# Moving 50 bfloat16 transposes of a gated attention and FFN block from TensorE to the DMA queue

## The chip, the cores and the metric

The kernel runs on one core of a Trainium2 chip. The metric is the device time of one execution in microseconds (us); before the change it is 677.74 us, the median of 3 runs that lie between 677.37 and 677.95. Engines are called as the profile calls them: PE is the matrix engine (PEld its weight loads), DVE the vector engine, ACT the scalar engine, POOL the general engine GpSimd. SP only issues DMAs here; ACT issues some too.

## The reference

The block takes x, 2 x 2048 tokens of 512 floats, and adds two gated branches. Cut to what matters:

```
x = x + tanh(g_xattn) * xattn(layernorm(x), ctx, mask, Wq, Wk, Wv, Wo)     # 16 heads, 77 keys
x = x + tanh(g_ffn)   * ffn(layernorm(x), clip_x, clip_down, w_gate, w_up, w_down)

def weight_fake_quant(w):           # one scale per row
    scale = max(abs(w), axis=1) / 127
    return clip(round(w / scale), -128, 127) * scale
def act_fake_quant(x, clip):        # one scale for the whole tensor
    scale = sigmoid(clip) * max(abs(x)) / 127
    return clip(round(x / scale), -128, 127) * scale
def ffn(x):
    xq   = act_fake_quant(x, clip_x)
    gate = xq @ weight_fake_quant(w_gate).T       # w_gate, w_up: 1408 x 512
    up   = xq @ weight_fake_quant(w_up).T
    h    = act_fake_quant(silu(gate) * up, clip_down)
    return h @ weight_fake_quant(w_down).T
```

The quantised integers are exact in bfloat16, so the matrix products of the FFN run on bfloat16 copies of them and the scales are put in afterwards.

## The kernel before

The tokens are 32 tiles of 128 rows, and x stays in SBUF (`x1`). The program is three blocks one after the other, each with its engines' instruction streams written out by hand, ordered by semaphores, and with all engines meeting between blocks.

**Attention block.** A slot loop (`tile_slots`) runs 36 slots; slot n holds the scores of tile n, the softmax transposes and outputs of tile n-1, the projection of tile n-2, the queries of tile n+2 and the transpose of tile n+4. Beside this, slots 0 to 21 quantise one chunk of 128 rows of w_gate (11 chunks) or w_up (11 chunks): SP loads the chunk (L305), DVE finds the rows' maxima and writes int8 (L581, L598), POOL makes the bfloat16 copy `w_bf` (L367). In the next slot PE transposes `w_bf` in four 128 x 128 pieces into the PSUM bank `p_x` (L845), and ACT copies the bank to `wgu` (L426). `p_x` is also the bank of the transposes of x (L728) and of the attention output (L804). There is one `w_bf`, so POOL waits for PE before it writes the next.

**Up block.** The tokens are taken in 8 groups of 4 tiles. A group has 11 steps; a step is 4 gate and 4 up matmuls of 512 columns (L1157), a Silu on ACT (L1042), a product and a maximum on DVE (L1118, L1122). During steps 0, 2, 4 and 6 of group g ACT quantises the four tiles of group g+1 to int8 (L1013), POOL makes the bfloat16 copy in one of two buffers `xqb` (L1007), PE transposes it after steps 2, 4, 6 and 8 (L1147) into the PSUM banks `p_t`, and ACT copies it to one of two buffers `xqT` in steps 3, 5, 7 and 9 (L1018). The four tiles of group 0 go the same way in a prologue, with DVE in POOL's and ACT's place. In groups 0 and 1 w_down is quantised and transposed too (L1028, L1169, L1034). The products h of groups 0 to 3 don't fit in SBUF beside those of the last four: SP writes each to memory after its group (L995).

**Down block.** 32 tiles of h are quantised and multiplied with w_down; ACT reads the spilled ones back.

SP's queue is in order: an instruction that waits for its semaphore holds all behind it. In the up block it holds only the loads of w_down and the four spills.

Of the kernel before, what the change touches and what calls it, by code (L numbers as in the profile page):

```python
# [7 lines left out]
BF16 = mybir.dt.bfloat16  # L8
# [7 lines left out]
P = 128  # L16
# [3 lines left out]
KD = D // P  # L20
# [6 lines left out]
NT = B * S // P  # L27
# [11 lines left out]
NS = 4  # L39
# [16 lines left out]
def flamingo_block(nc, x, ctx_in, mask, g_xattn, g_ffn, Wq, Wk, Wv, Wo, clip_x, clip_down,  # L56
# [6 lines left out]
    with top:  # L63
# [30 lines left out]
        with attn:  # L94
# [17 lines left out]
            with work:  # L112
# [103 lines left out]
                t_wT = sem("t_wT")  # L216
# [22 lines left out]
                a_wT = sem("a_wT")  # L239
# [57 lines left out]
                def _(sp):  # L297
                    def weights(k):
                        return k.rearrange("(k p) n -> p k n", p=P)

                    def rows(w):
                        if w:
                            sp.wait_ge(v_wi8, w)
                        src = (w_gate if w < KI else w_up)[w % KI * P:(w % KI + 1) * P, :]
                        sp.dma_start(w_in[:, :], src).then_inc(d_w, 16)  # L305
# [20 lines left out]
                    sp.dma_start(x1[:, 8:12, :], x_v[:, 8:12, :]).then_inc(l_x[3], 16)  # L326
                    for w in range(2, NW):
                        rows(w)

                @block.gpsimd  # L330
                def _(pool):
# [25 lines left out]
                    def slot(n, t):  # L357
# [4 lines left out]
                        if runs(n, NW):  # L362
                            wait(pool, v_wam, n + 1)
                            wait(pool, v_wi8, n + 1)
                            wait(pool, t_wT, n)
# [21 lines left out]
                def _(act):  # L387
# [16 lines left out]
                    def slot(n, t):  # L404
# [17 lines left out]
                        if runs(n - 1, NW):  # L422
                            wait(act, t_wT, n)

                            w = n - 1
                            act.copy(wgu[:, span(w // KI), :, span(w % KI * P, P)]  # L426
                                     .rearrange("p a k i -> p (a k) i"),
                                     p_x[:, :, 0:P // 2].bitcast(BF16)).then_inc(a_wT, 1)
# [288 lines left out]
                def _(pe):  # L717
# [101 lines left out]
                    def slot(n, t):  # L819
# [18 lines left out]
                        if runs(n - 1, NW):  # L838
                            wait(pe, g_wbf, n)
                            if isinstance(n, int) and n == 1:  # L840
                                pe.wait_ge(idb, 1)
                            wait(pe, v_olo, n - 1)
                            wait(pe, v_xlo, n + 4)
                            for k in range(KD):
                                last = pe.transpose(p_x[:, k, 0:P // 2].bitcast(BF16), w_bf[:, k * P:(k + 1) * P],  # L845
                                                    identb[:, :])
                            last.then_inc(t_wT, 1)
# [6 lines left out]
                        if runs(n + 4, NT):  # L854
                            wait(pe, v_olo, n - 1)
                            wait(pe, a_wT, n if not isinstance(n, int) else min(n, NW))
# [41 lines left out]
        with ffn:  # L898
# [10 lines left out]
            with up:  # L909
# [44 lines left out]
                c_xqT = sem("c_xqT")  # L954
                a_warm = sem("a_warm")
# [34 lines left out]
                def _(sp):  # L990
                    for r in range(KD):
                        sp.dma_start(wd_raw[:, r, :], w_down[r * P:(r + 1) * P, :]).then_inc(l_wd[r], 16)
                    for g in range(NG - NS):
                        sp.wait_ge(v_h, KI * (g + 1))
                        sp.dma_start(h_spill[g * TG:(g + 1) * TG].rearrange("t p n -> p t n"),  # L995
                                     h[:, g * TG:(g + 1) * TG, :, :].rearrange("p t k n -> p t (k n)"))\
                          .then_inc(h_out[g], 16)
# [4 lines left out]
                def _(pool):  # L1002
                    pool.memset(ones[:, :], 1.0).then_inc(g_one, 1)
                    for n in range(TG, NT):
                        pool.wait_ge(a_xq8, n + 1)
                        pool.wait_ge(t_t, n - 1)
# [3 lines left out]
                def _(act):  # L1010
# [4 lines left out]

                    def place(n, j, t):
                        wait(act, t_t, n + 1)
                        act.copy(xqT[j][:, :, t * P:(t + 1) * P], p_t[t % 2][:, 0:KD, :]).then_inc(c_xqT, 1)  # L1018
# [18 lines left out]
                    def group(g, j, slot):  # L1037
                        for i in range(KI):
# [103 lines left out]
                def _(pe):  # L1142
# [7 lines left out]
                    def group(g, j, slot):  # L1150
                        wait(pe, c_xqT, g * TG + TG)
                        for i in range(KI):
# [8 lines left out]
                            if more(g) and i in (2, 4, 6, 8):  # L1161
                                tile_transpose(g * TG + TG + i // 2 - 1, i // 2 - 1)
# [195 lines left out]
```

## Time and profile before

| | us |
|---|---|
| median of 3 runs | 677.74 |
| the profiled execution | 677.35 |
| its span, first to last instruction | 675.6 |
| PE busy | 646.6 (96%) |
| DVE busy | 510.5 (76%) |
| ACT busy | 357.4 (53%) |
| POOL busy | 169.4 (25%) |
| 16 DMA engines, mean of the two data queues | 14.9% + 6.8% |

The profiled execution is 1.75 us longer than its span; that part lies outside the instructions. The attention block fills the span up to about 413 us, the up block up to about 588 us, the down block the rest. Busy PE includes matmuls that overlap one another, so a slot's period, start to start, says more than its busy time.

### The profile page before, as it was taken

What the parts mean: (1) busy time and instruction counts of PE and PEld (TensorE: products, weight loads), DVE (VectorE), ACT (ScalarE), POOL (GpSimd) and SP (SyncE); (2) the same over time, 40 slices, a digit from 0 to 9 for tenths busy, and PEclk for the clock granted to TensorE, in tenths of its full rate; (3) what the DMA queues carried; (4) which work ended last, traced back from release to release, by engine and by line L of the source; (5) the groups of instructions that cost most, each with busy time, mean ns of one, the idle gap of its engine ahead of it and who ended that gap; (6) DMA issues with size and microseconds to landing.
All of it is one profiled execution on the core that took longest, in us unless ns stands there. A gap on an engine that the chain in (4) does not pass through costs nothing. (4 is left out here: it accounts for less than half of the span.)

```text
span 675.6 us, 13440 instructions
## 1 busy us (share of the span) xinstructions
PE 646.6 (96%) x4209; PEld 493.3 (73%) x4235; DVE 510.5 (76%) x947; ACT 357.4 (53%) x561; POOL 169.4 (25%) x374
## 2 busy tenths in 40 slices
PE   6789999999999999999999996999999999899997
PEld 6588999999999999999999994444444444354443
DVE  4687878878787878867776755799777788865764
ACT  1555455555554555654453433578666655354653
POOL 5122222223232222211110111111111110046875
PEclk9999999999999999999999998899999999999999
DMA  6258010101000010000000002231344000079723
GB/s 229 85 172 324 22 32 18 31 16 31 16 18 28 16 31 16 17 1 1 1 2 1 1 0 82 91 155 48 141 173 171 0 0 1 0 286 384 281 111 122
DMA packets 22488, 53.29 MB, mean 79 GB/s; under 512 B 4884, under 2 KB 5038, under 8 KB 22446
## 3 DMA queue, kind: packets, MB, share of 16 engines
q1 hardware_dynamic: 16654, 35.96, 14.9%
q10 hardware_dynamic: 5792, 16.80, 6.8%
q8 instruction: 23, 0.38, 0.2%
q14 instruction: 19, 0.16, 0.1%
HBM read 32.50 MB, written 19.92 MB: 78 GB/s over the span
## 5 line engine op out<-in xcount | busy, mean ns | idle before, releaser
L522 DVE TENSOR_REDUCE sb_smax<-ps_s 128x8 f32<-128x616 f32 x64 | 51.1, 798 | 64.6 <-PE ps_s L759 64.4
L1157 PE MATMUL ps_u<-sb_xqT,sb_wgu 128*128 128x512 bf16 x349 | 90.2, 380 | 0.2
L1157 PE MATMUL ps_g<-sb_xqT,sb_wgu 128*128 128x512 bf16 x338 | 89.2, 382 | 1.2 <-DVE sb_xqT L1129 0.5
L1042 ACT ACTIVATE sb_silu<-ps_g,sb_sgu 128x512 f32<-128x512 f32 x88 | 60.5, 688 | 55.0 <-PE ps_g L1157 46.4
L421 ACT COPY sb_pT<-ps_p 128x512 f32<-128x512 f32 (+1 forms) x96 | 46.4, 521 | 70.0 <-PE ps_p L770 70.0
L1118 DVE SCALAR_TENSOR_TENSOR sb_h<-ps_u,sb_sgu,sb_silu 128x512 f32<-128x512 f32 (+1 forms) x88 | 65.9, 749 | 20.4 <-PE ps_u L1157 19.5
L720 PE MATMUL ps_q<-sb_xT_hi,sb_wq_hi 128*128 128x256 f32 x256 | 77.6, 303 | 2.1 <-DVE sb_q_lo L513 1.5
L781 PE MATMUL ps_o<-sb_vblk,sb_pT 128*128 (+4 forms) x640 | 79.0, 270 | 0.1
L781 PEld LDWEIGHTS ps_o<-sb_vblk,sb_pT 128*128 128x128 f32 (+1 forms) x640 | 76.8, 191 | 0.6 <-ACT sb_pT L421 0.3
L1330 PE MATMUL ps_z<-sb_wdT,sb_hq 128*128 128x512 bf16 x344 | 76.0, 379 | 0.6
L722 PE MATMUL ps_q<-sb_xT_hi,sb_wq_lo 128*128 128x256 f32 x256 | 72.4, 283 | 0.0
L721 PE MATMUL ps_q<-sb_xT_lo,sb_wq_hi 128*128 128x256 f32 x256 | 72.3, 282 | 0.0
L1242 POOL TENSOR_TENSOR sb_wgu<-sb_wgu,sb_x 128x512 f32<-128x512 f32 x31 | 54.3, 1755 | 53.5 <-DVE sb_wgu L1287 53.5
L1122 DVE TENSOR_REDUCE sb_hmax<-sb_h 128x1 f32<-128x512 f32 (+1 forms) x88 | 60.4, 686 | 7.6
L1157 PEld LDWEIGHTS ps_u<-sb_xqT,sb_wgu 128*128 128x128 bf16 x352 | 34.6, 98 | 42.0 <-issue 1.0
L409 ACT CAST sb_oT_hi<-ps_x 128x512 fp32r<-128x512 f32 x31 | 18.3, 589 | 88.6 <-PE ps_x L804 88.6
L1330 PEld LDWEIGHTS ps_z<-sb_wdT,sb_hq 128*128 128x128 bf16 x352 | 34.1, 98 | 42.3 <-ACT sb_hq L1257 1.9
L1257 ACT CAST sb_hq<-sb_h 128x1408 bf16<-128x1408 int8 x32 | 43.6, 1365 | 35.5 <-DVE sb_h L1281 35.5
L1157 PEld LDWEIGHTS ps_g<-sb_xqT,sb_wgu 128*128 128x128 bf16 x352 | 32.9, 98 | 34.1 <-DVE sb_xqT L1129 0.8
L528 DVE TENSOR_TENSOR sb_prob<-ps_s,sb_smax 128x616 f32<-128x616 f32 x64 | 51.0, 797 | 3.0
L720 PE MATMUL ps_y<-sb_wo_hi,sb_oT_hi 128*128 128x512 f32 x124 | 51.3, 414 | 0.9 <-DVE sb_wo_lo L604 0.9
L349 POOL TENSOR_TENSOR sb_ve<-sb_mvt,sb_eps 128x1 f32<-128x1 f32 x32 | 6.1, 191 | 180.6 <-DVE sb_mvt L584 180.6
(160 smaller groups left out, 1419.9 us busy)
## 6 DMA issues: line engine op xcount, KB each, us to landing
h_spill<-sb_h SPq DMA_DIRECT2D x4, 2816.0 KB, 8.6
sb_h<-h_spill ACTq DMA_DIRECT2D x16, 704.0 KB, 6.2
out_dram<-sb_wgu SPq DMA_DIRECT2D x32, 256.0 KB, 2.0
sb_x<-in_x_dram ACTq DMA_DIRECT2D x1, 4096.0 KB, 16.1
sb_w_in<-in_L_ffn_w_gate_dram SPq DMA_DIRECT2D x11, 256.0 KB, 2.7
sb_w_in<-in_L_ffn_w_up_dram SPq DMA_DIRECT2D x11, 256.0 KB, 2.6
sb_h<-in_L_ffn_w_down_dram SPq DMA_DIRECT2D x4, 704.0 KB, 5.9
sb_x<-in_x_dram SPq DMA_DIRECT2D x2, 1024.0 KB, 11.7
```

What stands on the lines that cost most here:

```text
L522: dve.tensor_reduce(smax[:, half, :].rearrange("p (g h) -> p g h", g=2), half_scores(), X, ALU.max).then_inc(v_max, 1)
L528: dve.tensor_tensor(prob[t % 2][:, half, :].rearrange("p (g h m) -> p g h m", g=2, h=HG), half_scores(), smax[:, half, :].rearrange("p (g ...
L720: pe.matmul(o, hi, rhi, start=first, stop=False)
L721: pe.matmul(o, hi, rlo, start=False, stop=False)
L722: return pe.matmul(o, lo, rhi, start=False, stop=last)
L781: last = pe.matmul(p_o[:, first:end + 1, :].rearrange("p h d -> p (h d)"), pT[rows, half * KB + j, :], vblk[rows, span(b), half, SLOT0[j]: ...
L1042: act.activation(silu[(j * KI + i) % 2][:, :, :].rearrange("p t n -> p (t n)"), p_g[(j * KI + i) % 2][:, :], ACT.Silu, scale=sgu[:, i:i + ...
L1118: dve.scalar_tensor_tensor(steps_h, p_u[(j * KI + i) % 2][:, :, :], sgu[:, KI + i:KI + i + 1], silu[(j * KI + i) % 2][:, :, :], ALU.mult, ...
L1122: dve.tensor_reduce(hmax[:, span(u)], steps_h, mybir.AxisListType.XY, ALU.max, apply_absolute_value=True).then_inc(v_hmax, 1)
L1157: last = pe.matmul(banks[(j * KI + i) % 2][:, :], wgu[:, what, k, i * P:(i + 1) * P], xqT[j][:, k, :], start=(k == 0), stop=(k == KD - 1))
L1242: pool.tensor_tensor(yd[k], yd[k], x1[:, span((v + RT) % NT), :].rearrange("p a d -> p (a d)"), ALU.add).then_inc(g_out, 1)
L1330: last = pe.matmul(p_z[k % 4][:, :], hq[k % 4][:, i, :], wdT[:, i, :], start=(i == 0), stop=(i == KI - 1))
```

## The change

The transposes of the weight chunks, and of the 28 token tiles of groups 1 to 7, are no longer done by PE and copied by ACT. SP issues one DMA transpose for each instead, which reads the 128 x 512 bfloat16 tile (128 KB) in SBUF and writes it transposed to its place in `wgu` or `xqT`, as 128 partitions of 4 rows of 128 elements. As built, such an instruction names blocks of 16 source partitions by 128 columns, 32 of them. POOL now waits for the DMA before it writes over `w_bf` or `xqb`; PE waits for it at the start of groups 1 to 7. SP's stream in the up block becomes: four transposes of group 1, spill of group 0, four transposes of group 2, spill of group 1, and so on. The prologue's four tiles and w_down stay on PE.

```diff
@@ SP, attention block
+                    def rows_transposed(w):
+                        sp.wait_ge(g_wbf, w + 1)
+                        sp.dma_start_transpose(wgu[:, w // KI, :, w % KI * P:(w % KI + 1) * P], w_bf[:, :])\
+                          .then_inc(d_wT, 16)
...
+                    rows_transposed(0)
                     for w in range(2, NW):
                         rows(w)
+                        rows_transposed(w - 1)
+                    rows_transposed(NW - 1)
+                    sp.wait_ge(d_wT, 16 * NW)
@@ POOL, attention block
-                            wait(pool, t_wT, n)
+                            wait(pool, d_wT, 16 * n)
@@ ACT, attention block
-                        if runs(n - 1, NW):
-                            wait(act, t_wT, n)
...
-                            act.copy(wgu[:, span(w // KI), :, span(w % KI * P, P)]
...
@@ PE, attention block
-                        if runs(n - 1, NW):
-                            wait(pe, g_wbf, n)
...
-                                last = pe.transpose(p_x[:, k, 0:P // 2].bitcast(BF16), w_bf[:, k * P:(k + 1) * P],
...
-                            wait(pe, a_wT, n if not isinstance(n, int) else min(n, NW))
@@ SP, up block
+                    def tiles_transposed(g):
+                        if g >= 2:
+                            sp.wait_ge(t_u, KI * (g - 1))
+                        for t in range(TG):
+                            n = g * TG + t
+                            sp.wait_ge(c_xqb, n + 1)
+                            sp.dma_start_transpose(xqT[g % 2][:, :, t * P:(t + 1) * P], xqb[n % 2][:, :])\
+                              .then_inc(d_xqT[n % 2], 16)
+
+                    for g in range(1, NG):
+                        tiles_transposed(g)
+                        if g <= NG - NS:
+                            f = g - 1
+                            sp.wait_ge(v_h, KI * (f + 1))
+                            sp.dma_start(h_spill[f * TG:(f + 1) * TG].rearrange("t p n -> p t n"),
...
@@ POOL, up block
-                        pool.wait_ge(t_t, n - 1)
+                        if n < TG + 2:
+                            pool.wait_ge(t_t, n - 1)
+                        else:
+                            pool.wait_ge(d_xqT[n % 2], 16 * ((n - TG) // 2))
@@ ACT, up block
-                            if more(g) and i in (3, 5, 7, 9):
-                                if i == 3:
-                                    wait(act, t_u, g * KI)
-                                place(g * TG + TG + (i - 3) // 2, 1 - j, (i - 3) // 2)
@@ PE, up block
-                        wait(pe, c_xqT, g * TG + TG)
+                        if isinstance(g, int) and g == 0:
+                            pe.wait_ge(c_xqT, TG)
+                        else:
+                            for i in range(2):
+                                pe.wait_ge(d_xqT[i], g * (16 * TG // 2))
...
-                            if more(g) and i in (2, 4, 6, 8):
-                                tile_transpose(g * TG + TG + i // 2 - 1, i // 2 - 1)
```

On PE in a slot of the attention block (L770 are the last transposes of probabilities, L720 to L722 the next queries) the program before has these rows:

```order
L770 MATMUL ps_p0<-sb_identf,sb_prob1 128x128
L770 MATMUL ps_p0<-sb_identf,sb_prob1 104x128
L845 MATMUL ps_x<-sb_identb,sb_w_bf 128x128 x4
L720 MATMUL ps_q<-sb_xT_hi0,sb_wq_hi 128x256
L721 MATMUL ps_q<-sb_xT_lo0,sb_wq_hi 128x256
```

and the changed one, at the same place:

```order
L771 MATMUL ps_p0<-sb_identf,sb_prob1 128x128
L771 MATMUL ps_p0<-sb_identf,sb_prob1 104x128
L721 MATMUL ps_q<-sb_xT_hi0,sb_wq_hi 128x256
L722 MATMUL ps_q<-sb_xT_lo0,sb_wq_hi 128x256
L723 MATMUL ps_q<-sb_xT_hi0,sb_wq_lo 128x256
```

The four transposes of `w_bf` are gone and nothing else moved. On PE in steps 1 to 4 of a group, before (ps_g and ps_u are the gate and up banks, ps_t that of the tile transposes):

```order
L1157 MATMUL ps_g0<-sb_xqT0,sb_wgu 128x512 x4
L1157 MATMUL ps_u0<-sb_xqT0,sb_wgu 128x512 x4
L262 REGISTER_ALU x2
L1147 MATMUL ps_t0<-sb_identb,sb_xqb0 128x128 x4
L262 REGISTER_ALU
L1157 MATMUL ps_g1<-sb_xqT0,sb_wgu 128x512 x4
L1157 MATMUL ps_u1<-sb_xqT0,sb_wgu 128x512 x4
```

and in the changed program:

```order
L1161 MATMUL ps_g0<-sb_xqT0,sb_wgu 128x512 x4
L1161 MATMUL ps_u0<-sb_xqT0,sb_wgu 128x512 x4
L261 REGISTER_ALU
L1161 MATMUL ps_g1<-sb_xqT0,sb_wgu 128x512 x4
L1161 MATMUL ps_u1<-sb_xqT0,sb_wgu 128x512 x4
```

The steps follow one another with no transposes between them. On SP in the up block the queue before is:

```order
L992 DMA sb_h<-in_L_ffn_w_down_dram 128x1408 x4
L995 DMA h_spill<-sb_h 128x4x1408 [waits v_h] x4
L909 UNCONDITIONAL_BRANCH [waits h_out2,h_out3,h_out1,h_out0]
```

and the changed one begins:

```order
L983 DMA sb_h<-in_L_ffn_w_down_dram 128x1408 x4
L990 DMA_TRANSPOSE sb_xqT<-sb_xqb 128x4x128 [waits c_xqb] x4
L998 DMA h_spill<-sb_h 128x4x1408 [waits v_h]
L990 DMA_TRANSPOSE sb_xqT<-sb_xqb 128x4x128 [waits c_xqb,t_u]
L990 DMA_TRANSPOSE sb_xqT<-sb_xqb 128x4x128 [waits c_xqb] x3
L998 DMA h_spill<-sb_h 128x4x1408 [waits v_h]
```

A spill now stands between the transposes of one group and those of the next, and the first transpose after it goes out while the spill's bytes are moving.

## Rows read from the trace of the kernel before

**Rows 1.** Windows: us; PE, PEld, DVE, ACT, POOL busy; clock, DMA share, GB/s.

```profile
100.00:200.00 100.00, 100.00 (x770) 95.69 (x770) 80.46 (x171) 53.17 (x92) 25.64 (x84) 1.00 0.08 21
494.86:514.75 19.89, 19.79 (x104) 9.52 (x105) 15.71 (x23) 12.27 (x21) 2.46 (x4) 1.00 0.36 147
```

**Rows 2.** Timeline of PE, attention: start us, us, engine, line, instruction.

```profile
105.83 0.39 PE L845 MATMUL ps_x<-sb_identb,sb_w_bf 128*128 128x128 bf16 x4
...
117.60 0.39 PE L845 MATMUL ps_x<-sb_identb,sb_w_bf 128*128 128x128 bf16 x4
...
311.66 0.30 PE L757 MATMUL ps_s<-sb_k_hi,sb_q_hi 128*128 128x308 f32 x1
...
323.16 0.30 PE L757 MATMUL ps_s<-sb_k_hi,sb_q_hi 128*128 128x308 f32 x1
```

**Rows 3.** Timeline of PE, up block, around two of the transposes.

```profile
509.57 1.03 PE L1157 MATMUL ps_g<-sb_xqT,sb_wgu 128*128 128x512 bf16 x4
...
514.75 0.39 PE L1147 MATMUL ps_t<-sb_identb,sb_xqb 128*128 128x128 bf16 x4
...
534.63 0.39 PE L1147 MATMUL ps_t<-sb_identb,sb_xqb 128*128 128x128 bf16 x4
```

**Rows 4.** Groups by line: busy us, mean ns | idle before, its releaser.

```profile
L1147 PE MATMUL ps_t<-sb_identb,sb_xqb 128*128 128x128 bf16 x128 | 12.6, 222 | 1.5 <-DVE sb_xqb L1135 1.5
L1018 ACT COPY sb_xqT<-ps_t 128x512 bf16<-128x512 bf16 x28 | 16.2, 579 | 0.0
L426 ACT COPY sb_wgu<-ps_x 128x512 bf16 (+1 forms) x22 | 12.9, 588 | 2.7 <-issue 2.7
L1118 DVE SCALAR_TENSOR_TENSOR sb_h<-ps_u,sb_sgu,sb_silu 128x512 f32<-128x512 f32 (+1 forms) x88 | 65.9, 749 | 20.4 <-PE ps_u L1157 19.5 <-ACT sb_silu L1042 0.3
L1122 DVE TENSOR_REDUCE sb_hmax<-sb_h 128x1 f32<-128x512 f32 (+1 forms) x88 | 60.4, 686 | 7.6
```

**Rows 5.** Timeline of POOL: the casts of one group's four tiles.

```profile
512.16 0.61 POOL L1007 CAST sb_xqb<-sb_xq 128x512 bf16<-128x512 int8 x1 [8.54 <-ACT sb_xq L1013]
515.53 0.61 POOL L1007 CAST sb_xqb<-sb_xq 128x512 bf16<-128x512 int8 x1 [2.76 <-ACT sb_xq L1013]
519.21 0.61 POOL L1007 CAST sb_xqb<-sb_xq 128x512 bf16<-128x512 int8 x1 [3.06 <-ACT sb_xq L1013]
522.89 0.61 POOL L1007 CAST sb_xqb<-sb_xq 128x512 bf16<-128x512 int8 x1 [3.06 <-ACT sb_xq L1013]
```

**Rows 6.** DMA issues: KB each, median us from issue to landing.

```profile
h_spill<-sb_h SPq DMA_DIRECT2D x4, 2816.0 KB, 8.6
...
out_dram<-sb_wgu SPq DMA_DIRECT2D x32, 256.0 KB, 2.0
```

**Rows 7.** Window in the spill of group 0, columns as in Rows 1.

```profile
450.00:452.00 2.00, 2.00 (x11) 0.88 (x9) 1.97 (x5) 1.84 (x4) 0.61 (x1) 1.00 1.01 411
```

**Rows 8.** Tile vblk: SBUF to SBUF copies, ns on SP's queue, min/median/max.

```profile
L322 SPq DMA_DIRECT2D sb_vblk<-sb_pT x12: 644/830/1040, 30.9 to 40.4; - x12
```

**Rows 9.** Timeline of SP: the spill of group 0.

```profile
448.77 0.38 SPq L995 DMA_DIRECT2D h_spill<-sb_h  x1
```

**Rows 10.** Timeline of PE: the start of group 1.

```profile
447.49 1.03 PE L1157 MATMUL ps_g<-sb_xqT,sb_wgu 128*128 128x512 bf16 x4
```

**Rows 11.** Timeline of POOL: the casts of chunks 1 and 2.

```profile
48.78 0.61 POOL L367 CAST sb_w_bf<-sb_w_i 128x512 bf16<-128x512 int8 x1
...
59.46 2.75 POOL L367 CAST sb_w_bf<-sb_w_i 128x512 bf16<-128x512 int8 x1
```

**Rows 12.** DMA issues between 28 and 50 us.

```profile
sb_x<-in_x_dram SPq DMA_DIRECT2D x1, 1024.0 KB, 8.7
...
sb_vblk<-sb_pT SPq DMA_DIRECT2D x4, 39.7 KB
...
sb_vblk<-sb_pT SPq DMA_DIRECT2D x1, 0.5 KB
```

**Rows 13.** Timeline of ACT's queue: the load of 4 MB of x.

```profile
50.93 0.39 ACTq L446 DMA_DIRECT2D sb_x<-in_x_dram  x1
```

More of the change, by code:

```diff
@@ L215, in flamingo_block @@
                 t_y = sem("t_y")
-                t_wT = sem("t_wT")
+                d_wT = sem("d_wT")
                 v_st = sem("v_st")
@@ L238, in flamingo_block @@
                 a_ohi = sem("a_ohi")
-                a_wT = sem("a_wT")
                 g_self = sem("g_self")
@@ L421, in slot @@
                                 act.copy(pT[:, k0:k1, :], p_p[c % 2][:, 0:k1 - k0, :]).then_inc(a_p, 1)
-                        if runs(n - 1, NW):
-                            wait(act, t_wT, n)
-                            w = n - 1
-                            act.copy(wgu[:, span(w // KI), :, span(w % KI * P, P)]
-                                     .rearrange("p a k i -> p (a k) i"),
-                                     p_x[:, :, 0:P // 2].bitcast(BF16)).then_inc(a_wT, 1)
                         for half in range(2):
@@ L837, in slot @@
                             prob_transpose(n - 1, (t - 1) % 4, 2)
-                        if runs(n - 1, NW):
-                            wait(pe, g_wbf, n)
[L840 to L844, printed above, removed]
-                                last = pe.transpose(p_x[:, k, 0:P // 2].bitcast(BF16), w_bf[:, k * P:(k + 1) * P],
-                                                    identb[:, :])
-                            last.then_inc(t_wT, 1)
                         if runs(n + 2, NT):
@@ L954, in flamingo_block @@
                 c_xqT = sem("c_xqT")
+                d_xqT = [sem(f"d_xqT{i}") for i in range(2)]
                 a_warm = sem("a_warm")
@@ L992, in _ @@
                         sp.dma_start(wd_raw[:, r, :], w_down[r * P:(r + 1) * P, :]).then_inc(l_wd[r], 16)
[L993 to L997, printed above, removed]
+                    def tiles_transposed(g):
[12 more added lines that the diff above has]
+                            sp.dma_start(h_spill[f * TG:(f + 1) * TG].rearrange("t p n -> p t n"),
+                                         h[:, f * TG:(f + 1) * TG, :, :].rearrange("p t k n -> p t (k n)"))\
+                              .then_inc(h_out[f], 16)
+                    for i in range(2):
+                        sp.wait_ge(d_xqT[i], 16 * (NT - TG) // 2)
                     for g in range(NG - NS):
@@ L1014, in quantise @@
                                        bias=nbq[:, span(n)], scale=rsq[:, span(n)]).then_inc(a_xq8, 1)
-                    def place(n, j, t):
-                        wait(act, t_t, n + 1)
-                        act.copy(xqT[j][:, :, t * P:(t + 1) * P], p_t[t % 2][:, 0:KD, :]).then_inc(c_xqT, 1)
                     def down_part(u):
@@ L1150, in group @@
                     def group(g, j, slot):
-                        wait(pe, c_xqT, g * TG + TG)
+                        if isinstance(g, int) and g == 0:
+                            pe.wait_ge(c_xqT, TG)
+                        else:
+                            for i in range(2):
+                                pe.wait_ge(d_xqT[i], g * (16 * TG // 2))
                         for i in range(KI):
```

## Prediction

> **What bounds the kernel now.** I read the page first, for the share of each engine over the span, then windows by stage, then the timeline of PE slot by slot. The reader is to see that PE is the bound in both stretches that the change touches: in 100 us of attention PE is busy all 100, in a group of the up block 19.79 of 19.89, with DVE next at 80% and 79% [rows 1]. Busy PE overlaps itself, so I go by periods. A slot of attention with a weight transpose in it takes 117.60 - 105.83 = 11.77 us; a late slot, where the chunks are done, takes 323.16 - 311.66 = 11.50 us [rows 2]. A middle group takes 534.63 - 514.75 = 19.88 us, and three steps without a transpose between them take 514.75 - 509.57 = 5.18 us, 1.727 us a step [rows 3]; eleven such steps are 19.0 us. So the transposes stand on the path, at their issue cost and not at their latency: the 222 ns that the table by line gives for one [rows 4] is four times too much.
>
> **What is removed.** Attention: 22 sets of four transposes, 0.27 us a set, if the slot with its chunk becomes as short as one without. DVE still has its work on the chunk in these slots, so the late slot is not quite the same thing; but at 80% of a slot of 11.77 us it has 2.3 us to spare, and PE gives up only 0.27. 22 x 0.27 = 5.9 us. The first three slots are paced by loads and by other engines, so I count 21: 5.6 us. Up block: 19.88 - 19.0 = 0.88 us a group, for four sets, so 0.22 us a set; 28 sets make 6.1 us. Sum of the two: 11.7 us. ACT loses 28 copies of 0.579 us and 22 of 0.588 us [rows 4], 29 us of its work, of which I count nothing: PE covers it.
>
> **What is added, and its price.** Fifty DMA transposes of 128 KB, none of which the trace shows. Two numbers matter: how long one holds the queue or the DMA engines so that the next can't run (S), and how long until POOL and PE may go on (L). Lower bound of S: the bytes at the 411 GB/s at which the spill moves [rows 7], 128 KB / 411 = 0.32 us. For the rest the nearest rows are the twelve SBUF to SBUF copies with short rows: SP's queue was held between 644 and 1040 ns by one [rows 8], and their sizes run from 0.5 KB to 39.7 KB [rows 12]; with rows of 4 x 33 floats cut into runs of 132 bytes, the largest has 308 runs, so a run costs (1040 - 644) / 304 = 1.3 ns above a fixed 0.64 us. A transpose read as 512 pieces of 256 bytes (four to a partition) is then 0.64 + 0.67 = 1.3 us; one paid by the 32-byte pieces that a block of 16 rows leaves on each destination partition, 128 x 4 x 8 = 4096 pieces, is 0.64 + 5.3 = 6.0 us. I take S = 1.3 us, because the copies whose rows I lean on are also counted by the run that is read, and keep 0.32 and 6.0 as the ends. Latency on top: a 256 KB store lands in 2.0 us [rows 6], of which its bytes are 0.64, so 1.4 us fixed; L = S + 1.4 = 2.7 us.
>
> Does that fit? In the up block I lay the four tiles against the group's start at 509.57 [rows 3]. Their casts end at 3.2, 6.6, 10.3 and 13.9 us [rows 5]; with the transposes gone from PE the last two come at 10.0 and 13.5. A transpose goes out at each; the last lands at 13.5 + 2.7 = 16.2, and the next group starts at 19.0: 2.8 us to spare. POOL's new wait, for the DMA two tiles back, is long met at an interval of 3.5 us. Behind it on POOL stand only the later casts, and for them wait SP, and PE at the next group's first matmul.
>
> In groups 1 to 4 a spill is in the way. It goes out 448.77 - 447.49 = 1.3 us after the group's start [rows 9, 10] and lands 8.6 us later [rows 6], so its bytes leave the engines some 9.2 us into the group. The transposes of tiles 0 and 1 are queued behind it and land at 9.2 + 2.7 = 11.9 and 13.2. Tile 2's cast waits for the first, ends at 12.5 and lands at 15.2; tile 3 is at 13.5 to 13.8 and lands at 16.5. Still 2.5 us early. The spill itself isn't delayed: SP has issued its four transposes by 13.8 and the spill's own condition comes 1.3 us into the next group, as before.
>
> In attention one transpose must land within a slot. POOL holds its next cast for it, behind that cast stand POOL's small statistics for the tiles five ahead, and DVE's next int8 write waits for the cast. L = 2.7 against 11.5 us leaves nothing to pay. The worst place is the start: chunk 0's transpose is queued on SP behind the 1 MB load of x that takes 8.7 us to land [rows 12], so it lands near 52 to 54, and POOL's cast of chunk 1, at 48.78 before, waits 4 us or so; chunk 2's cast was at 59.46 [rows 11], and beside the 4 MB load that ACT issues at 50.93 [rows 13] its wait may hold POOL a few us again. POOL's statistics are needed a slot later, so I count 0, and up to 2 us as the bound.
>
> Two pages of the Trainium skill speak on S, against each other. "VectorE: DVE Perf Modes", section "The three transpose paths", gives 1309 ns for one 128 x 128 bfloat16 transpose by DMA, against 390 ns on TensorE; taken four times it is an estimate of 5.2 us a tile, near my upper end. "Advanced Engine Details and Errata", section "X-Bar Transpose (TRN2)", says that such transposes are as fast as regular DMAs, which is my lower end. No row here shows which.
>
> **The sum.** The profiled execution is 677.35 us, span 675.6 and 1.75 around it. 677.35 - 5.6 - 6.1 = 665.65. The median of the runs lies 0.4 above that execution, so the forecast is 666.0 us. Its own range is 664 to 669: down by the full 22 slots and by up to 1 us where PE waits for ACT's part of w_down in groups 0 and 1, up by the 2 us of the start.
>
> **Rivals.** First, *the queue becomes the bound of the up block*. SP and the DMA engines take one transpose after another; a group can't be shorter than the first cast, four times S and the landing: 3.2 + 4S + 1.4. That reaches the 19.0 us of a group at S = 3.6, and has eaten the 11.7 us won at S = 4.0 (7 groups x 1.6 = 11.2). At S = 6.0 a group takes 28.6 us, 9.6 more, 67 us over 7 groups. In groups 1 to 4 the spill goes out as the fourth transpose leaves the queue, about 1.4 us before the group starts, and takes 7 us, so the first transpose starts at 5.6 instead of 3.2: 2.4 x 4 = 10 us. Sum 666 + 77 = 743 us. For it: 4096 short pieces, and nothing else on the DMA queues is written transposed. Against it: 6.0 needs a price by the piece written. Attention stays free of it, since 7.4 us is still under a slot. The page's 5.2 us, an estimate, would give 6.5 x 7 and the same 10, some 722 us.
>
> Second, *only the last tile is late*. S is small but a landing takes longer than my 2.7. The last tile has 19.0 - 13.5 = 5.5 us. Behind a spill the margin is smaller, because tile 3's cast waits for tile 1: tile 1 lands at 9.2 + 1.3 + L, the cast takes 0.6, tile 3 lands L later, 11.1 + 2L, which is 19.0 at L = 4.0. At L = 4.5 that is 20.1, 1.1 us in each of four groups: 670.4. At L = 6 it is 23.1, 4.1 us each, and 0.5 us in each of the other three groups: 16.4 + 1.5 = 18 us, 684. For it: the spill takes 8.6 us to land; against it: that is 2.8 MB, and 256 KB take 2.0.
>
> Third, *another engine holds the pace*, so that PE's saving comes out as waits. DVE's pair per step is 749 + 686 ns [rows 4], 1.44 us of 1.73, and in attention it keeps 2 us of a slot. Steps without a transpose run at 1.727 already, so the up block can't lose this way; attention could. Half of its 5.6 us lost gives 669; all of it 671.6.
>
> **Chances.** Forecast 0.63. Another engine's pace 0.05; the last tile late 0.08 (0.06 still faster, 0.01 the same, 0.01 slower); the queue as the bound 0.24, of which 0.02 with S between 3.6 and 4.0, still faster, and 0.01 at no difference. A difference of 0.2%, 1.4 us, is about what a measurement of this kernel can tell. Faster 0.63 + 0.05 + 0.06 + 0.02 = 0.76, same 0.02, slower 0.22. The range reaches from 663 over the small stalls and the near part of the first rival: to 700, where S is 4.6 and some 0.17 lie beyond.
>
> **What would show it.** Right: slots 1 to 21 at 11.5 us, groups 1 to 6 at 19.0, no idle PE at a group's first gate matmul, DMA transposes that land within 4 us. The first rival: PE idle at the first matmul of each of groups 1 to 7 with a DMA transpose as the releaser, evenly long, and SP's queue busy from the first cast on. The second: such waits in the groups with a spill and hardly elsewhere. The third: PE idle inside steps, released by DVE. The prediction is wrong if one transpose occupies the queue for over 3.6 us.

## The result, and the profile after

The changed kernel takes 665.15 us, the median of 4 runs (665.15 to 665.65), and the kernel before in the same rounds 677.83 us (677.37 to 677.95). The ratio is 0.982 with a 95% interval of 0.980 to 0.984: 12.7 us or 1.9% less by the medians, 0.85 us below the forecast of 666.0. The profiled execution took 665.65 us, with a span of 663.9 against 675.6, which is 11.7 us; it is the longest of the four runs, and the other three lie at 665.15 and 665.16.

The page of the changed kernel first, its sums per engine and the line of the DMA packets:

```profile
PE 634.2 (96%) x4035; PEld 479.8 (72%) x4035; DVE 507.3 (76%) x947; ACT 331.9 (50%) x511; POOL 166.5 (25%) x374
...
DMA packets 49687, 59.83 MB, mean 90 GB/s; under 512 B 32084, under 2 KB 32238, under 8 KB 49646
```

ACT lost 25.5 us of work, PE 174 recorded instructions (200 were removed; the trace of the kernel before lacks some), and the share of PE did not move. Before, there were 22,488 packets, of which 4,884 under 512 bytes. The difference of 27,199 over 50 transposes is 544 packets each. By their sizes in the trace, 512 of them carry 256 bytes and 32 carry 4 bytes; a plain DMA such as the spill also has such 4-byte packets, 16 of them.

The windows of the changed kernel, columns as in [rows 1]: 100 us of attention, groups 0 and 1, and group 3.

```profile
100.00:200.00 100.00, 100.00 (x759) 95.84 (x758) 82.71 (x176) 50.78 (x88) 27.04 (x86) 1.00 0.14 34
...
419.14:440.78 21.64, 20.45 (x108) 9.44 (x108) 19.23 (x37) 13.84 (x23) 2.45 (x4) 1.00 0.19 49
440.78:463.17 22.39, 21.10 (x116) 9.63 (x114) 21.66 (x42) 16.68 (x31) 2.45 (x4) 1.00 0.59 153
482.17:501.17 19.00, 19.00 (x90) 8.63 (x89) 15.72 (x23) 10.37 (x16) 2.45 (x4) 1.00 0.56 181
```

Group 3 takes 19.00 us in place of 19.89 [rows 1, 3]. Groups 0 and 1 are longer, and here the rows of before that the prediction did not look at are needed. The same two windows of the kernel before:

```profile
424.72:447.49 22.77, 22.33 (x122) 10.79 (x124) 19.22 (x37) 15.77 (x27) 2.46 (x4) 0.95 0.05 22
447.49:469.79 22.30, 21.71 (x130) 10.69 (x130) 21.66 (x42) 18.46 (x34) 2.46 (x4) 1.00 0.32 130
```

Group 1 took 22.30 us and now takes 22.39. In both kernels DVE is busy 21.66 of it. Group 0 fell from 22.77 to 21.64, but its granted clock was 0.95 and is 1.00.

In attention a slot with a chunk in it now takes what a late one takes. PE's timeline of the changed kernel, the same score matmul in two slots that follow one another, early and then late:

```profile
103.85 0.39 PE L758 MATMUL ps_s<-sb_k_hi,sb_q_hi 128*128 x1
...
115.33 0.39 PE L758 MATMUL ps_s<-sb_k_hi,sb_q_hi 128*128 x1
...
306.11 0.30 PE L758 MATMUL ps_s<-sb_k_hi,sb_q_hi 128*128 128x308 f32 x1
...
317.62 0.30 PE L758 MATMUL ps_s<-sb_k_hi,sb_q_hi 128*128 128x308 f32 x1
```

The slots take 115.33 - 103.85 = 11.48 us and 317.62 - 306.11 = 11.51, against 11.77 and 11.50 [rows 2]. Twenty slots changed in this way, the first of them at 64.77 us.

What a transpose costs, from the entries of the two source tiles `w_bf` and `xqb` (ns on SP's queue, min/median/max, first and last start; then the landing):

```profile
L302 SPq DMA_TRANSPOSE sb_wgu<-sb_w_bf x22: 1190/1196/1632, 43.2 to 279.5; - x22
...
DMA to landing us min/median/max: 2.3/2.4/9.4
...
L990 SPq DMA_TRANSPOSE sb_xqT<-sb_xqb x28: 1188/1191/2373, 422.4 to 552.7; - x28
...
DMA to landing us min/median/max: 2.4/2.5/9.1
```

S is 1.19 us where 1.3 was taken, L is 2.4 to 2.5 us where 2.7 was. The 8 to 9 us are the first transposes behind a spill, and the first three in attention, which go out beside the loads of x.

Where they are waited for, in the changed kernel's waits (us in total, times, longest us), of the stretch from 20 to 300 us and then of the up block:

```profile
POOL sb_swgu L374 <- DMA sb_wgu<-sb_w_bf: 16.4, 3, 8.7
```

```profile
POOL sb_xqb L1015 <- DMA sb_xqT<-sb_xqb: 20.1, 4, 6.2
...
ACT sb_wd_bf L1032 <- DVE sb_wd_i L1103: 9.7, 10, 1.8
...
PEld ps_w L1171 <- ACT sb_wd_bf L1032: 4.5, 5, 1.1
```

POOL waits 36.5 us in all for transposes, and none of it reaches PE: the first slots end at the same microsecond in both kernels (below), and no first gate matmul of a group waits for a DMA.

Laid side by side, the span's 11.7 us come from these places (start of PE's work in each, us):

| stretch | before | after | gain |
|---|---|---|---|
| to the slot at 64.77 | 64.77 | 64.77 | 0 |
| from there to the last projections of attention | 341.71 | 336.17 | 5.54 |
| to the start of group 0 | 18.24 | 18.20 | 0.04 |
| group 0 | 22.77 | 21.64 | 1.13 |
| group 1 | 22.30 | 22.39 | -0.09 |
| groups 2 to 6 | 99.44 | 94.97 | 4.47 |
| group 7 | 20.99 | 21.00 | 0 |
| down block | 85.38 | 84.76 | 0.62 |

### The profile page after: what moved, and what is told of

Read it like the earlier page. It is cut to its first block and busy times, and to the rows that moved or that the text cites. A ratio compares the mean times of both kernels' runs of the same rounds, so it can differ in the third digit from the quotient of the medians.

```text
span 663.9 us, 12956 instructions
## 1 busy us (share of the span) xinstructions
PE 634.2 (96%) x4035; PEld 479.8 (72%) x4035; DVE 507.3 (76%) x947; ACT 331.9 (50%) x511; POOL 166.5 (25%) x374
## 5 line engine op out<-in xcount | busy, mean ns | idle before, releaser
L722 PE MATMUL ps_q<-sb_xT_lo,sb_wq_hi 128*128 128x256 f32 x256 | 72.2, 282 | 0.0
```

What stands on the lines that cost most here:

```text
L722: pe.matmul(o, hi, rlo, start=False, stop=False)
```

## Experiments

### Each half alone

The first kernel has the attention block of the changed kernel and the up block of the one before, the second the reverse.

```diff
@@ the first, against the kernel before (attention block alone)
+                        rows_transposed(w - 1)
...
@@ the second, against the changed kernel (attention block alone)
-                        rows_transposed(w - 1)
...
+                        if runs(n - 1, NW):
+                            wait(pe, g_wbf, n)
...
```

> Only the attention block is the changed one; the up block is that of before. Theory (PE's issue time is what is saved): attention gives back 0.27 us in each of 19 to 20 slots, so the first matmul of group 0 starts 5.5 us sooner than before, and the kernel takes 677.8 - 5.5 = 672.3 us (671.5 to 673.0). The groups take 19.89 us as before. Rival (ACT's relief of 22 copies is the cause): the same time, but slots would be shorter than 11.50 us. Rival (the difference before to after is chance in the clock at a block's start): under 1 us from attention, 676 to 678.

> Only the up block is the changed one; attention is that of before. Theory, as mended by the trace of the changed kernel: groups 2 to 6 are 0.89 us shorter each, 4.45 us; groups 0 and 1 gain nothing, because DVE with w_down paces them (group 1: DVE busy 21.66 of 22.4 us in both kernels). So 677.8 - 4.45 = 673.4 us, give or take 1.2 us of clock at the block's start (672.0 to 674.0). As the prediction had it (28 sets, groups 0 and 1 too): 6.1 us, 671.7. Additive with e1: the two gains sum to 10 to 11 us, and what is missing to the 12.7 us measured is clock after the block borders.

Measured: attention alone 670.30 us (669.42 to 672.74, 6 runs), a ratio of 0.991 (0.989 to 0.993); the up block alone 672.91 us (670.77 to 673.35, 6 runs), 0.993 (0.991 to 0.995); before in the same rounds 677.42 us (675.42 to 678.11, 11 runs). That is 7.1 and 4.5 us. The second came out as expected; the first lies below its range of 671.5 to 673.0. In the profiled executions the attention stretch of the first is 336.15 us, 5.56 less than before, as expected; its groups 2 to 6, with the old up block, are at 19.89 us, and yet its group 0 takes 21.64 us instead of 22.77. That was not expected. It also shows that the removal of the transposes gives nothing in group 0, since here they are still on PE. The second has groups 2 to 6 at 19.00 us, group 0 at 23.35 and group 1 at 22.42.

What group 0 gained is the clock. PE's timeline at the start of group 0, before:

```profile
424.72 1.89 PE L1157 MATMUL ps_g<-sb_xqT,sb_wgu 128*128 128x512 bf16 x4 [0.52 <-DVE sb_xqT L1129]
```

and in the changed kernel:

```profile
419.14 1.04 PE L1161 MATMUL ps_g<-sb_xqT,sb_wgu 128*128 128x512 bf16 x4 [0.52 <-DVE sb_xqT L1129]
```

The same four matmuls, 1.89 us at a granted clock of 0.50 (1.2 GHz) and 1.04 us at 1.00 (2.4 GHz). Windows of 1 us ahead of the group, columns as in [rows 1], in the kernel before:

```profile
420.72:421.72 1.00, 0.37 (x4) 0.17 (x4) 0.44 (x2) 1.00 (x3) 0.00 (x0) 1.00 1.07 428
423.72:424.72 1.00, 0.48 (x4) 0.22 (x4) 0.58 (x2) 0.00 (x0) 0.00 (x0) 0.50 1.03 428
```

and in the changed one:

```profile
415.14:416.14 1.00, 0.93 (x4) 0.05 (x2) 0.43 (x1) 1.00 (x3) 0.00 (x0) 0.50 1.06 411
418.14:419.14 1.00, 0.40 (x5) 0.23 (x5) 0.78 (x3) 0.00 (x0) 0.00 (x0) 1.00 0.98 406
```

At the border of the blocks PE idles some 5 us in both and then works with gaps. Before, the clock had come back 4 us ahead of the group and had fallen again 1 us ahead of its start; in the changed kernel it came back later and stayed. In the second kernel above, with the old attention block, it stayed at 0.50 from the border until at least 4 us into group 0, whose 23.35 us go with that. The work at the border is the same in all; why the clock comes out differently stays open.

### Dummy transposes put back on PE

The changed kernel, with four transposes of the identity matrix after steps 2, 4, 6 and 8, which nobody reads and nobody waits for.

```diff
+                            if more(g) and i in (2, 4, 6, 8):
+                                for k in range(KD):
+                                    pe.transpose(p_t[(i // 2 - 1) % 2][:, k, :], identb[:, :], identb[:, :])
```

> The changed kernel, with four extra PE transposes of identb into the unused banks p_t after steps 2, 4, 6 and 8 of groups 0 to 6, where the tile transposes stood; nothing waits for them and ACT copies nothing. Theory (PE's issue time): groups 2 to 6 return to 19.89 us, 4.45 us in all; groups 0 and 1 stay as they are, DVE paces them; 665.2 + 4.45 = 669.6 us (669.2 to 670.6). Rival (the gain came from ACT's missing copies or from the removed waits between PE and ACT): groups stay near 19.0 and the time near 665.2.

Measured: 670.18 us (669.36 to 672.65, 6 runs), a ratio of 0.990 (0.988 to 0.992), as the theory had it. Groups 2 to 6 are back at 19.88 to 19.90 us, groups 0 and 1 stay at 21.64 and 22.40. PE's timeline around one set in group 2, starts and us:

```profile
466.37 1.03 PE L1161 MATMUL ps_g<-sb_xqT,sb_wgu 128*128 128x512 bf16 x4
...
468.10 0.39 PE L1167 MATMUL ps_t<-sb_identb 128*128 128x128 bf16 x4
468.32 1.03 PE L1161 MATMUL ps_g<-sb_xqT,sb_wgu 128*128 128x512 bf16 x4
```

The gate matmuls of one step and the next start 468.32 - 466.37 = 1.95 us apart, 0.22 more than a step of 1.727 [rows 3]. The price in groups 2 to 6 is PE's issue time alone: no data, no ACT copy and no wait belongs to these dummies. In groups 0 and 1 eight such sets are issued as well and cost nothing. There PE has the room.

### A dearer transpose, twice and four times

Each tile of groups 1 to 7 is transposed two or four times, the extra copies into unused room of h. This asks how near the first rival was. The lines are those of four times; twice has `range(2 - 1)`.

```diff
...
+                            for k in range(4 - 1):
+                                sp.dma_start_transpose(room[:, k * D:(k + 1) * D].rearrange("p (k n) -> p k n", k=KD),
+                                                       xqb[n % 2][:, :]).then_inc(d_xqT[n % 2], 16)
```

> The changed kernel, but each tile of groups 1 to 7 is transposed twice by DMA, once to unused room in h first; POOL and PE wait for both. A transpose held SP's queue 1.2 us and landed in 2.4 us, so one tile now holds it 2.4 us (S = 2.4) and lands 3.6 us after its cast. Theory (the prediction's chain): groups 5 and 6 stay at 19.0 us, since casts come 3.45 us apart and the last lands at 13.5 + 3.6 = 17.1. Groups 2 to 4 have a spill whose bytes leave at 9.2: tile 0 ends at 11.6, tile 1 at 14.0 and lands at 15.2, tile 3's cast ends at 15.8, it starts at 16.4, ends at 18.8 and lands at 20.0: 1.0 us more in each, 3 us in all, 668 us (666 to 669.5). Rival (a transpose occupies the DMA engines less than it holds the queue, or the spill and the transposes overlap): 665 to 665.5, no group longer.

> The changed kernel, but each tile of groups 1 to 7 is transposed four times by DMA, three times to unused room in h first; POOL and PE wait for all four. One tile holds the queue 4 x 1.2 = 4.8 us, which is beyond the prediction's point of 3.6 us where the queue becomes the bound. Theory: a group without a spill takes 3.2 + 4 x 4.8 + 1.2 = 23.6 us, 4.6 more than 19.0 (groups 5 and 6); one with a spill, which goes out 1.2 us before the group starts and takes 7 us, 5.8 + 19.2 + 1.2 = 26.2 us, 7.2 more (groups 2 to 4), 3.8 more for group 1 at 22.4, 2 more for group 0 at 21.6. Sum 9.2 + 21.6 + 3.8 + 2 = 37 us: 702 us (690 to 710), with PE idle at the first matmul of each group. Rival (only the landing counts, transposes of one tile overlap on the engines): L about 3 to 4 us, no group over 20 us, under 668 us.

Measured, twice: 667.48 us (666.54 to 670.15), a ratio of 0.987 (0.985 to 0.990). Groups 2 to 6 take 19.74, 19.78, 19.00, 18.99 and 19.00 us, and the two long ones end in PE's wait for a transpose:

```profile
482.22 1.03 PE L1167 MATMUL ps_g<-sb_xqT,sb_wgu 128*128 128x512 bf16 x4 [0.58 <-DMA sb_xqT<-sb_xqb]
...
502.00 1.03 PE L1167 MATMUL ps_g<-sb_xqT,sb_wgu 128*128 128x512 bf16 x4 [0.61 <-DMA sb_xqT<-sb_xqb]
```

This is the second rival, the last tile late behind a spill, at twice the real price. It came out at 0.8 us in two groups where 1.0 was expected in three: in group 4 the third cast came 10.6 us after the group's start and the last tile was in time, in group 3 it came after 11.7.

Four times: 719.55 us (718.87 to 720.75), a ratio of 1.064 (1.061 to 1.066). The expected 702 us was missed by 17. SP's queue in group 5, start and us (the sets of three are the extra copies):

```profile
560.85 3.81 SPq L994 DMA_TRANSPOSE sb_h<-sb_xqb  x3
564.70 1.27 SPq L996 DMA_TRANSPOSE sb_xqT<-sb_xqb  x1
...
571.30 3.88 SPq L994 DMA_TRANSPOSE sb_h<-sb_xqb  x3
...
576.54 3.88 SPq L994 DMA_TRANSPOSE sb_h<-sb_xqb  x3
580.46 1.27 SPq L996 DMA_TRANSPOSE sb_xqT<-sb_xqb  x1
```

Back to back a transpose holds the queue 1.27 us and the next starts 1.31 after it (576.54 - 571.30 = 5.24 for four), not the 1.19 of a lone one. So S was 5.24, not 4.8; four tiles at 0.44 us more in seven groups make 12 of the 17 us that were missed. And after a late start a group loses a second time. Its first matmul waited, and ran at half the clock:

```profile
556.73 1.88 PE L1167 MATMUL ps_g<-sb_xqT,sb_wgu 128*128 128x512 bf16 x4 [5.29 <-DMA sb_xqT<-sb_xqb]
```

Its window (us; PE, PEld, DVE, ACT, POOL busy; clock, DMA share, GB/s):

```profile
556.73:560.00 3.27, 3.27 (x8) 1.15 (x9) 0.00 (x0) 1.27 (x2) 0.00 (x0) 0.50 0.00 0
```

The first transpose starts 560.85 - 556.73 = 4.1 us into the group. With four times 5.24 and 1.3 us more to the landing that is 4.1 + 21.0 + 1.3 = 26.4 us, and the group takes 26.38. The form of the first rival is thus shown, first cast plus 4S plus landing; had one transpose of the up block cost what this set of four does, the kernel would have become 6% slower.

What holds the next transpose back is the issuing, not the 16 DMA engines. From 560.85 to 581.73 us SP's queue has no gap over 0.2 us, and in a window of this stretch the engines are busy half of the time (columns as above):

```profile
570.00:580.00 10.00, 8.64 (x40) 3.72 (x38) 8.26 (x13) 4.13 (x6) 0.61 (x1) 1.00 0.53 104
```

These numbers also weigh a page that spoke for the upper price. The Trainium skill, "VectorE: DVE Perf Modes", "The three transpose paths", gives 1309 ns for one 128 x 128 transpose by DMA. Here 1.19 to 1.27 us is the queue time of a whole 128 x 512 tile, four such squares: the figure is near what one instruction takes, and the estimate of 5.2 us a tile, which took it four times, does not hold.

### The groups that gained nothing

If DVE holds the pace of groups 0 and 1, taking work from it must shorten them. POOL writes the 12 int8 chunks of w_down in DVE's place; POOL is slower at it but busy only 2.45 us of a group.

```diff
-                            dve.tensor_scalar(wd_i8[c % 2][:, 0:cols.stop - cols.start], wd_raw[:, r, cols],
-                                              wd_inv[:, r:r + 1], QMAX, ALU.mult, ALU.mult).then_inc(v_wd8, 1)
...
+                        pool.tensor_scalar(wd_i8[c % 2][:, 0:cols.stop - cols.start], wd_raw[:, r, cols],
+                                           wd_inv[:, r:r + 1], QMAX, ALU.mult, ALU.mult).then_inc(v_wd8, 1)
...
```

> The changed kernel, with the 12 scalings of w_down to int8 moved from DVE to POOL, which is idle for most of groups 0 and 1. Theory (DVE paces groups 0 and 1): DVE loses 12 x 0.46 = 5.4 us there, 21.66 of 22.4 us become 19 in group 1; PE then paces: 19.0 us and 6 sets of w_down transposes at 0.22, 20.3 us a group, so the two groups take 40.6 to 41.5 instead of 44.0 us, and the kernel 662 us (661.5 to 663.5). Against it: POOL is in order, and in group 1 its cast of tile 2 waits until the spill is through, 11.7 us into the group, with a w_down chunk behind it; that may give back 1 to 2 us. Rival (the hand-over of chunks between DVE, ACT and PE paces these groups, not DVE's busy time): no gain, or a loss, since POOL takes longer for a chunk: 665 to 668.

Measured: 661.79 us (661.53 to 663.71, 5 runs), a ratio of 0.9785 (0.976 to 0.981) to the kernel before. Its windows of groups 0 and 1:

```profile
418.86:438.93 20.07, 19.96 (x106) 9.67 (x109) 17.60 (x33) 14.40 (x24) 6.31 (x10) 1.00 0.21 56
438.93:459.32 20.39, 20.29 (x115) 10.01 (x115) 19.07 (x34) 16.68 (x30) 6.29 (x10) 1.00 0.63 169
```

DVE's work falls by 1.63 and 2.59 us, the groups by 1.57 and 2.00, and PE is now busy all but 0.1 us of them. The rival, that the hand-over of the chunks from engine to engine paced these groups, expected no gain or a loss, since POOL takes longer for a chunk; it falls. Eleven steps of 1.727 us and the 5 and 7 sets of w_down's transposes that PE has in these groups, at 0.22 us, make 20.1 and 20.5 us, near what they now take: PE's issue time is the bound here too, once DVE is relieved. The twelve operations cost DVE 455 ns and POOL 657 ns each, by the tables by line of the changed kernel and of this one:

```profile
L1103 DVE TENSOR_SCALAR sb_wd_i<-sb_h,sb_wd_inv 128x512 int8<-128x512 f32 (+1 forms) x12 | 5.5, 455 | 0.0
```

```profile
L1015 POOL TENSOR_SCALAR sb_wd_i<-sb_h,sb_wd_inv 128x512 int8<-128x512 f32 (+1 forms) x12 | 7.8, 657 | 4.6 <-DVE sb_swd L1113 4.3 <-ACT sb_wd_bf L1049 0.2
```

This is the fastest kernel of the study.

### w_down's chunks by DMA too

With DVE relieved, the 12 sets of w_down's transposes are on PE's path. The next kernel gives them to the DMA queue as well; the bfloat16 chunks lie in unused room of h.

```diff
+                    def chunk_transposed(c):
+                        r, q = divmod(c, WC)
+                        n = wd_cols(q).stop - wd_cols(q).start
+                        sp.wait_ge(a_wdb, c + 1)
+                        sp.dma_start_transpose(wdT[:, 4 * q:4 * q + n // P, r * P:(r + 1) * P],
+                                               wd_room[:, c * D:c * D + n]).then_inc(d_wd, 16)
...
-                                    last = pe.transpose(p_w[c % 2][:, k, :], wd_bf[c % 2][:, k * P:(k + 1) * P],
-                                                        identb[:, :])
...
```

> The kernel of the last experiment (POOL quantises w_down), with w_down's 12 chunks also transposed by DMA from SBUF, so that PE loses 12 sets of four transposes and ACT 12 copies. If the transposes of w_down cost PE what those of the tiles did, 0.22 us a set, and if neither DVE (17.6 and 19.07 us busy in groups 0 and 1) nor the queue takes over: groups 0 and 1 at 19.0 and 19.1 to 19.3 us instead of 20.07 and 20.39, the kernel 2.2 us below it, near 659.7 (659 to 661.5). The rival: in group 1 the chunks' transposes queue with those of the tiles behind spill 0, the last chunk lands late, and DVE waits for it at the start of group 2: group 2 above 19.3 us, and no gain or a loss of up to 2 us, 662 to 664.

Measured: 662.96 us (662.32 to 665.75, 5 runs), a ratio of 0.981 (0.979 to 0.983). That is no gain on the kernel of the last experiment: groups 0 to 2 take 59.89 us together instead of 59.45. Group 0 did fall, from 20.07 to 19.19 us. Groups 1 and 2 rose, from 20.39 and 18.99 to 20.94 and 19.76; 0.86 us of group 1 is the wait at its end, and of the rest, 20.08, DVE is busy 19.57, so that PE had little more to win there. PE's waits at the start of group 2:

```profile
459.43 1.03 PE L1185 MATMUL ps_g<-sb_xqT,sb_wgu 128*128 128x512 bf16 x4 [0.86 <-DMA sb_xqT<-sb_xqb]
464.50 1.04 PE L1185 MATMUL ps_u<-sb_xqT,sb_wgu 128*128 128x512 bf16 x4 [0.59 <-DVE sb_h L1139]
```

and SP's queue in group 1, from the spill on:

```profile
439.99 0.40 SPq L1017 DMA_DIRECT2D h_spill<-sb_h  x1
440.50 8.28 SPq L1005 DMA_TRANSPOSE sb_wdT<-sb_h  x3
448.82 1.27 SPq L995 DMA_TRANSPOSE sb_xqT<-sb_xqb  x1
...
455.37 2.58 SPq L995 DMA_TRANSPOSE sb_xqT<-sb_xqb  x2
457.99 3.88 SPq L1005 DMA_TRANSPOSE sb_wdT<-sb_h  x3
```

The rival named for this run holds. Three chunks and the spill stand ahead of the first tile, the queue is never empty from 440.5 to 461.9, tile 3 lands late, and DVE waits for the last chunk in group 2. DVE's timeline there:

```profile
463.70 0.75 DVE L1139 SCALAR_TENSOR_TENSOR sb_h<-ps_u,sb_sgu,sb_silu 128x512 f32 x1 [2.75 <-PE ps_u L1185]
```

The idle time is put down to PE's bank, which had long been filled; the wait that ends last is that for the last chunk's transpose. Queue time has an end. Thirteen transposes stand between two spills here: the first three were issued while the spill's bytes moved, until 448.8, and the other ten took 1.31 us each, 21.9 us in all from the spill on. By the same numbers a group of 19.0 us has room for three and then (19.0 - 8.8) / 1.31, seven more: an estimate of ten.

### Spills from another queue

Is a transpose late after a spill because it stands behind it in SP's queue? To see this, the four spills are issued by ACT.

```diff
+                            if i == 1 and 1 <= g <= NG - NS:
+                                f = g - 1
+                                act.wait_ge(v_h, KI * (f + 1))
+                                act.dma_start(h_spill[f * TG:(f + 1) * TG].rearrange("t p n -> p t n"),
...
-                            sp.dma_start(h_spill[f * TG:(f + 1) * TG].rearrange("t p n -> p t n"),
```

> The changed kernel, with the four spills issued by ACT, after the Silu of step 1 of groups 1 to 4, instead of by SP between the transposes. If a transpose lands late after a spill because it stands in the same ring behind it: POOL's waits for the DMA at tile 2 of groups 1 to 4 (6.16, 5.39, 4.53 and 4.07 us, 20.1 in sum) shrink to a fraction, and the first transposes land in 3 to 5 us. If it is because the 16 DMA engines themselves work off the spill first: both unchanged, about 9 us and 20 us. The time is the same either way, 665 (664 to 667), since PE waits for none of it.

> The changed kernel once more on this chip, so that the others are compared with it in the same rounds. Expected 665.2, profiled execution either near 665.6 or near 663.6, by whether the clock at the start of the down block is granted in full; groups 0 and 1 at 21.64 and 22.4 us, groups 2 to 6 at 19.0.

Measured: 665.13 us (664.91 to 665.54, 4 runs), against 665.60 us (665.28 to 668.13, 5 runs) for the changed kernel on the same chip. The time is the same, and so are the waits, or longer; POOL's line, of this kernel and then of the changed one on the same chip:

```profile
POOL sb_xqb L1009 <- DMA sb_xqT<-sb_xqb: 25.6, 4, 7.0
```

```profile
POOL sb_xqb L1015 <- DMA sb_xqT<-sb_xqb: 20.2, 4, 6.2
```

The transposes land within 10.2 us at most, against 9.2. So the place behind the spill in SP's queue is not what makes them late: the 16 DMA engines have the spill to move, whoever issued it. The packets in the two traces show how. In the first profile of the changed kernel not one of a transpose moves from 443 to 450 us, while the spill's go, and then they follow. With the spill in ACT's queue they begin at 448.1, and until 451.0 the two take turns, 192 packets of the spill (5632 bytes each) and 188 of the transposes (256 bytes); that gains the transposes nothing. Why none moves before 448.1, though the first was issued at 443.63, stays open. A window of this kernel after the spill (issued at 442.95) and the first transpose (443.63), in which the engines are full:

```profile
446.00:448.00 2.00, 1.36 (x9) 0.53 (x8) 1.93 (x5) 0.87 (x3) 0.61 (x1) 1.00 1.01 414
```

## Why the prediction came out right

**The bound.** PE's issue time set both stretches, in attention and in groups 2 to 6. The dummies show it for groups 2 to 6: put back without any data, they cost what the real ones did, 0.22 us a set and not the 222 ns each of the table by line. In attention no dummies were put back; there it rests on PE being busy all of 100 us in both kernels.

**Attention, 5.6 us.** Measured 5.54 us, in 20 slots of 0.28 us where 21 of 0.27 were counted; the slots before them gave nothing, since both kernels reach the same point at 64.77 us. POOL's wait at the start was 8.7 us in the worst case, where 4 was guessed and then "a few us" more; POOL's statistics are needed a slot later, and the slack held.

**The up block, 6.1 us: the step that was off.** The prediction counted 28 sets at 0.22 us. Only the 20 of groups 2 to 6 gave it, 4.47 us; the 8 sets in groups 0 and 1 gave nothing. There DVE also quantises w_down and is busy 19.2 and 21.7 us, against 15.7 in a middle group, so its pace is what PE follows. The third rival said that another engine could hold the pace and then ruled it out for the up block with "Steps without a transpose run at 1.727 already, so the up block can't lose this way". That was read from a middle group and carried to all seven. The window of group 1 of the kernel before, above, would have shown it: 22.30 us with DVE at 97%. In group 0 DVE is at 89% and its pace reaches PE by the rows of waits shown above: PE's weight loads for `ps_w` wait for ACT's copy of the chunk, and this for DVE's int8 values (L1103). That POOL in DVE's place gives 3.6 us in just these two groups shows the cause.

**What made up for it.** This part is luck. 5.54 + 4.47 is 10.0 us from the transposes, 1.7 less than predicted, and the span fell by 11.7 all the same, because two other places gave 1.75 us that the prediction doesn't name. Of these, 1.13 us is group 0 at full clock instead of half in its first 2 us. Group 0 starts at full clock in all nine profiled executions with the new attention block, also with the old up block behind it, and in neither of the two with the old one. But in the later rounds the runs of the kernel before lie at two levels, 675.4 to 676.0 and 676.8 to 678.2 us, and those of the changed one at 665.3 to 665.6 with one at 668.1. So an execution may get the clock or not; no run here was made to tell, and the levels lie further apart than 1.13 us. The fastest runs of all rounds, 675.39 and 665.15, lie 10.2 us apart, near the 10.0 of the transposes. The last 0.62 us is the down block, which the change does not touch. In the nine profiled executions with the new attention block it took 84.70 to 84.76 us where the granted clock of its first 5 us was 1.00, and 84.89 to 85.06 where it was 0.66; but with the old one it took 85.38 at 0.66 and 85.37 at 1.00, so the clock is at most part of it. Both stay open. The medians lie another 1.0 us further apart than the spans; the stretch up to the slot at 64.77 us, equal in these two executions, took 64.07 to 65.03 us over all the profiled ones.

**The price of a DMA transpose.** S = 1.19 us against 1.3 taken, L = 2.4 to 2.5 against 2.7. The way to it, 512 runs of 256 bytes at 1.3 ns above 0.64 us [rows 8, 12], is borne out in its count: 512 packets of 256 bytes, not 4096. Its price for a run was not measured by itself. So the first rival falls. It needed S above 3.6 us, and the four-fold kernel shows what lay beyond. One step of the range was mis-added: by the rival's own sum S = 4.6 gives 704 us, and the upper end of 700 is reached at S = 4.5.

**The last tile behind a spill.** Predicted: tile 2's cast ends at 12.5 us into the group and tile 3's transpose lands at 16.2 to 16.5. POOL's casts in group 1 of the changed kernel:

```profile
443.76 0.61 POOL L1015 CAST sb_xqb<-sb_xq 128x512 bf16<-128x512 int8 x1 [9.49 <-ACT sb_xq L1021]
446.95 0.61 POOL L1015 CAST sb_xqb<-sb_xq 128x512 bf16<-128x512 int8 x1 [2.58 <-ACT sb_xq L1021]
453.73 0.61 POOL L1015 CAST sb_xqb<-sb_xq 128x512 bf16<-128x512 int8 x1 [6.16 <-DMA sb_xqT<-sb_xqb]
455.41 0.61 POOL L1015 CAST sb_xqb<-sb_xq 128x512 bf16<-128x512 int8 x1 [1.07 <-ACT sb_xq L1021]
```

Tile 2's cast starts 453.73 - 440.78 = 12.95 us into the group, a microsecond later than predicted, and tile 3's ends at 15.2; with 2.5 us to land it is there at 17.7, before the group's end at 22.39. In groups 2 to 4 the waits are shorter, 5.39, 4.53 and 4.07 us, and the last cast starts 12.9 us in, so its tile is there at 16.0, 3 us early. The reason given was half right: the transposes do follow the spill in the queue, but they are as late without that, because the same engines move the spill's bytes.

## What to carry to other kernels

Before a saving is multiplied by its count, read the window of each stretch in which it is counted: the stages of one loop can be bound by different engines, and here 8 of 28 sets lay in the two groups where DVE held the pace. For an operation that no trace showed, the number of pieces to be moved gave a price within 0.12 us here; its landing must be checked at the worst place, behind the largest transfer. Moving work to a DMA queue pays until the queue is full: two transposes a tile cost 1.5 us in all, four cost 54, and with w_down's chunks added there was nothing more to gain. Where a forecast comes out, add up the parts all the same: here two that nobody had counted hid one that was not there.

## What the runs showed of the hardware

A DMA transpose of a 128 x 512 bfloat16 tile from SBUF to SBUF held the issuing queue for 1.19 us when alone and 1.27 us in a row of them, starts 1.31 us apart, which is 131,072 bytes in 1.31 us or 100 GB/s, with the 16 engines busy 0.53 of the time; the spill moves at 411 GB/s with them busy throughout [rows 7]. The Trainium skill, "Advanced Engine Details and Errata", "X-Bar Transpose (TRN2)", says such transposes are as fast as regular DMAs. In landing that is near, 2.4 us for 128 KB against the 2.0 of a plain store of 256 KB [rows 6]. In throughput it does not hold against the spill. Against a plain copy in equally short runs nothing was measured; the copies of [rows 8, 12], in runs of 132 bytes, held the queue 1.04 us for 39.7 KB, which is slower still.

In the four-fold kernel PE's idle time behind a late transfer cost twice: the 5.3 us wait was followed by 3.3 us at a granted clock of 0.50, and the first transpose for the next group started 4.1 us into the group instead of 3.2.
